# Query and key projections, and their evictions, moved ahead in three of the eight steps of an attention loop

## The chip, the cores and the metric

One NeuronCore of a Trainium2 chip runs the whole program in one launch. The metric is the device time of that launch in microseconds (us), the median of several runs. All durations below are from one profiled execution of the kernel before.

## The reference

Three blocks follow one another on x of 4 batches x 1024 tokens x 128 channels, all in float32:

```python
x = x + 0.5 * ffn(layernorm(x))        # silu(gate) * up, 384 hidden, dequantized int weights
x = x + attn(layernorm(x))
x = x + 0.5 * ffn(layernorm(x))

# attn, 16 heads of 64
h = silu(x @ W1.T + b1) @ W2.T + b2
q, k, v = split(h @ Wg.T + bg)
dots = q @ k.T * 64 ** -0.5
dots = where(j >= i + 64, -inf, dots)  # a query sees the keys up to 63 places after itself
out = softmax(dots) @ v
attn = out @ Wo.T + bo
```

## The kernel before

The change lies in the attention. It runs 32 **turns**, one for each batch and pair of heads (A and B, 64 rows of the array each); the first and the last turn are written out, the 30 between them stand in a loop over two turns. A turn has eight **steps**, one for each tile of 128 queries. The order of the tiles (`at_step`) alternates narrow and wide ones, since the number of keys that a tile sees (`width`) grows with its place:

| step c | 0 | 1 | 2 | 3 | 4 | 5 | 6 | 7 |
|---|---|---|---|---|---|---|---|---|
| keys (width) | 192 | 1024 | 448 | 960 | 320 | 832 | 576 | 704 |
| job for the shared bank 7 | none | v0 | k0 | v1 | k1 | q0 | q1 | none |
| step whose groups are turned (c - 3) | 5 | 6 | 7 | 0 | 1 | 2 | 3 | 4 |
| groups of that step | 4 | 3 | 3 | 1 | 4 | 2 | 4 | 2 |

Every engine has its instructions written out in order, in a function `step` of its own, and starts them in that order; semaphores alone tie the engines together. What one step does, for step c:

- TensorE (PE), `step` at L914: `score` (L844) computes the scores of both heads, with each operand split into a high and a low part and so three matmuls for each head and part of up to 512 keys, into the only score banks there are. It waits for head B's exponentials of step c - 1, which read those banks (L850, L857); in steps 1, 3 and 5 the upper part (bank) can be written before that wait, because the step before it is narrow enough to lie in the lower bank. Then `turn` (L868) transposes the probabilities of step c - 3, four blocks of 128 to a group, the groups in turn into banks 4 and 5: group 0 and 1, called T0 and T1 here, and later T2 and T3. T2 can start once T0 has been copied out. Between T1 and T2 stand `project` (L775), which computes a job of the next turn (k0, k1, q0, q1) or of this one (v0, v1) into bank 7, once the job before it has been read out of that bank (`misc_read`, L826), and in even steps `output` (L833); in the odd steps `attend` (L886, probabilities times values) ends the step.
- VectorE (DVE), `step` at L683: `row_max` (L624) adds the mask and finds the negated maximum of each head; then `take` (L645) copies its groups (in steps 2, 4 and 6 that is T2) out of banks 4 and 5; then `invert` (L640), which waits for the exponentials of this very step; `add_output`; and last `queries_keys_low` (L581), the low part of a query or key projection out of bank 7, which waits for ScalarE's high part.
- ScalarE (ACT), `step` at L492: `take` of its groups 0 and 1 (L478; in steps 2, 4 and 6 both T0 and T1), then `exps` (L469), the exponentials of head A and head B, each after its maximum, then in steps 1, 3, 5 and 7 the attention's output, then `queries_keys` (L407), the high part of the projection out of bank 7, then the group 3.
- GpSimd (POOL) multiplies the probabilities of a step by the reciprocals of their sums (L387), after `invert`; it does this three steps ahead of the transposes.

The high and the low part of one projection are called its two evictions here: `qk_high` and `qk_done` are their semaphores. A job is run in a step's code only if the next turn exists, so the last turn has none of the k and q jobs. In an odd step an engine reaches `queries_keys` after `attention_out`.

```python
    JOBS = {1: "v0", 2: "k0", 3: "v1", 4: "k1", 5: "q0", 6: "q1"}
```

Of the kernel before, what the change touches and what calls it, by code (L numbers as in the profile page):

```python
# [36 lines left out]
def macaron(nc, x, w1t, b1, w2t, b2, wqkvt, bqk, bv, wot, bo, wgatet, wupt, wdownt, out):  # L37
# [34 lines left out]
    JOBS = {1: "v0", 2: "k0", 3: "v1", 4: "k1", 5: "q0", 6: "q1"}  # L72
# [13 lines left out]
    with ExitStack() as ctx:  # L86
# [114 lines left out]
        def taker(c, g):  # L201
            return int(g == 2) if c % 2 else g % 2
# [44 lines left out]
        def back(i, c, lag):  # L247

            return (i, c - lag) if c >= lag else (i - 1, c - lag + STEPS)
# [9 lines left out]
        def job_turn(job, i):  # L259

            return i + 1 if job[0] in "kq" else i - 1 if job in ("o1", "o2", "o3") else i

        def runs(job, carry, more):
            return more if job[0] in "kq" else carry or job not in ("o1", "o2", "o3")
# [139 lines left out]
        def _(act):  # L404
            give_credits(act, "scalar")

            def queries_keys(name, n, r, bank=MISC):  # L407

                kind, j = name[0], int(name[1])
                act.wait_ge(proj_qk.sem, proj_qk.after(name, n))  # L410
                nc.scalar.activation((qt if kind == "q" else kt)[r][0][:, j * BANK:(j + 1) * BANK], banks[:, bank, :], ACT.Identity,  # L411
                                     bias=bslot[r][:, 0:1] if kind == "q" else bslot[r][:, 1:2]).then_inc(qk_high.sem, 1)
# [56 lines left out]
            def exps(c, i):  # L469

                act.wait_ge(turned.sem, turned.after((c, groups[c] - 1), i - 1))
                for h in range(2):
                    act.wait_ge(maxed.sem, maxed.after(f"{c}{HEADS[h]}", i))
                    src = banks[:, SCORE[h]:SCORE[h] + 2, :].rearrange("p b n -> p (b n)")[:, 0:width[c]]
                    nc.scalar.activation(probs[c][:, h, :], src, ACT.Exp, bias=negmax[:, c, h:h + 1],  # L475
                                         accum_out=sums[:, c, h:h + 1]).then_inc(exped.sem, 1)

            def take(c, g, i):  # L478

                act.wait_ge(turned.sem, turned.after((c, g), i))  # L480
                act.wait_ge(attended.sem, attended.after(*two_back(i, c)))
                w = min(4, turns_in[c] - 4 * g)
                nc.scalar.activation(probst[c // 2 % 2][:, 4 * g:4 * g + w, c % 2 * P:(c % 2 + 1) * P],  # L483
                                     banks[:, TRANSPOSED[g % 2], 0:w * P].rearrange("p (t q) -> p t q", q=P), ACT.Copy).then_inc(taken[0].sem, 1)

            def attention_out(p, i):

                act.wait_ge(attended.sem, attended.after(p, i))
                act.wait_ge(wo_done.sem, wo_done.after(f"o{p}", i - 1))
                nc.scalar.activation(attn[:, p, :], banks[:, ATTEND, 0:2 * P], ACT.Copy).then_inc(attn_out.sem, 1)  # L490

            def step(c, i, r, carry=True, more=True):  # L492

                ti, tc = back(i, c, T_LAG)
                turning = carry or c >= T_LAG
                mine = [g for g in range(groups[tc]) if turning and taker(tc, g) == 0]
                for g in mine:
                    if g < 2:
                        take(tc, g, ti)
                exps(c, i)  # L500
                if c in ATTEND_AT and (carry or c >= PV_LAG):
                    for g in mine:
                        if g >= 2:
                            take(tc, g, ti)
                    attention_out(ATTEND_AT[c], i if c >= PV_LAG else i - 1)
                job = JOBS.get(c, "none")
                if job[0] in "kq" and runs(job, carry, more):
                    queries_keys(job, job_turn(job, i), 1 - r if job_turn(job, 0) else r)
                if c not in ATTEND_AT or not (carry or c >= PV_LAG):
                    for g in mine:  # L510
                        if g >= 2:
                            take(tc, g, ti)
# [23 lines left out]
        def _(dve):  # L536
# [87 lines left out]
            def row_max(c, i):  # L624

                lo, hi = hidden_keys[c]
                rows = banks[:, SCORE[0]:SCORE[0] + 4, :].rearrange("p (h b) n -> p h (b n)", h=2)
                dve.wait_ge(scored.sem, scored.after(f"{c}m" if EARLY[c] else f"{c}B", i))

                for heads in ([slice(0, 2)] if lo < BANK < hi else [slice(0, 1), slice(1, 2)]):  # L630
                    here = rows[:, heads, lo:hi]
                    hidden = mask[:, 0:hi - lo].unsqueeze(1).to_broadcast([P, here.shape[1], hi - lo])
                    last = nc.vector.tensor_tensor(here, here, hidden, ALU.add)  # L633
                last.then_inc(masked.sem, 1)
                dve.wait_ge(masked.sem, masked.after(c, i))
                for h in range(2):
                    dve.wait_ge(scored.sem, scored.after(f"{c}{HEADS[h]}", i))
                    nc.vector.tensor_reduce(negmax[:, c, h:h + 1], rows[:, h, 0:hi], AX.X, ALU.max, negate=True).then_inc(maxed.sem, 1)  # L638
# [44 lines left out]
            def step(c, i, r, carry=True, more=True):  # L683

                ti, tc = back(i, c, T_LAG)
                turning = carry or c >= T_LAG
                row_max(c, i)
                for g in range(groups[tc]):
                    if turning and taker(tc, g) == 1:
                        take(tc, g, ti)  # L690
                job = JOBS.get(c, "none")
                if job[0] == "v":
                    evict(job, i, r, carry, more)
                invert(c, i)
                if c in OUTPUTS:
                    evict(OUTPUTS[c], i, r, carry, more)
                if job[0] in "kq":
                    evict(job, i, r, carry, more)

            queries_keys_low("q0", 0, 0, FIRST["q0"])  # L700
# [26 lines left out]
        def _(pe):  # L727
# [47 lines left out]
            def project(name, n, r, bank=MISC):  # L775

                kind, j = name[0], int(name[1])
                if name == "k0":
                    pe.wait_ge(slots.sem, slots.after("b", n))
                w = wslot[r][:, "qkv".index(kind), :]  # L780
                bank = banks[:, bank, :]
                if kind != "v":
                    last = mm(bank, w, hslot[r][:, j * BANK:(j + 1) * BANK], start=True, stop=True)  # L783
                else:
                    for m in range(4):
                        toks = slice((4 * j + m) * P, (4 * j + m + 1) * P)
                        last = mm(bank[:, m * P:(m + 1) * P], hslot[r][:, toks], w, start=True, stop=True)  # L787
                last.then_inc((proj_v if kind == "v" else proj_qk).sem, 1)
# [120 lines left out]
            def turns_of(c, i, gs):  # L909
                for g in gs:  # L910
                    if g < groups[c]:
                        turn(c, g, i)

            def step(c, i, r, carry=True, more=True):  # L914

                ti, tc = back(i, c, T_LAG)
                turning = carry or c >= T_LAG
                attending = c in ATTEND_AT and (carry or c >= PV_LAG)

                score(c, i, r)  # L920
                if turning:
                    turns_of(tc, ti, (0, 1))
                job = JOBS.get(c, "none")
                if c in JOBS and runs(job, carry, more):
                    k = JOB_ORDER.index(job)
                    earlier = [name for name in JOB_ORDER[:k] if runs(name, carry, more)]
                    name, t = (earlier[-1], i) if earlier else (JOB_ORDER[-1], i - 1)
                    misc_read(name, job_turn(name, t))
                    if not carry and k == 0:
                        done(pe, pa.h, "h", CHUNKS - 1)  # L930
                    project(job, job_turn(job, i), 1 - r if job_turn(job, 0) else r)
                if turning and attending:
                    turns_of(tc, ti, (2, 3))
                if attending:
                    attend(ATTEND_AT[c], *((i, r) if c >= PV_LAG else (i - 1, 1 - r)))
                if c in OUTPUTS and runs(OUTPUTS[c], carry, more):
                    output(OUTPUTS[c], job_turn(OUTPUTS[c], i))
                if turning and not attending:
                    turns_of(tc, ti, (2, 3))
# [53 lines left out]
```

## Time and profile before

| | |
|---|---|
| runs of the kernel before | 1331.88 to 1333.56 us, median 1332.67 us (3 runs) |
| the profiled execution | 1333.85 us, of it 1331.2 us from the first instruction to the last (span) |
| granted TensorE clock, mean of the span | 0.997 of 2.4 GHz |
| TensorE matmuls busy | 1275.5 us (96%), 11250 instructions |
| TensorE weight loads busy | 978.4 us (73%) |
| GpSimd busy | 1155.0 us (87%) |
| VectorE busy | 924.5 us (69%) |
| ScalarE busy | 841.9 us (63%) |

The attention begins at 95.7 us of the span, with its first score, and its last score stands at 1259 us; before and after it run the feed-forward blocks. The profile puts every instruction under its line of the kernel, gives its start and duration, and for an engine that stood idle before an instruction it names what ended the wait. A matmul's duration holds a pipelined tail, so that the time that TensorE spends on a group is read from the start of one group to the start of the next.

### The profile page before, as it was taken

Reading aid. Unit: us, or ns where it says so; the run is one execution under the profiler, and the core shown is the slowest. Engines: PE = TensorE matmul, PEld = TensorE weight load, DVE = VectorE, ACT = ScalarE, POOL = GpSimd, SP = SyncE. Lnnn points to the kernel's source line nnn. Section 1 sums busy time; section 2 is a strip of 40 time slices with the busy share of each in tenths; the row PEclk is TensorE's granted clock in tenths of the full one; section 3 lists DMA queues with packets and bytes.
Section 4 is the critical chain, followed back from the end, with each engine's and each line's share of the span. In section 5 each row is a group of like instructions: output and inputs, shape, how many; then the busy total and the mean of one; then the engine's idle time right before and its main releaser. Section 6 shows DMA issues by size and latency. Waiting matters only on the chain.

```text
span 1331.2 us, 34824 instructions
## 1 busy us (share of the span) xinstructions
PE 1275.5 (96%) x11250; PEld 978.4 (73%) x11250; DVE 924.5 (69%) x2110; ACT 841.9 (63%) x1886; POOL 1155.0 (87%) x1090
## 2 busy tenths in 40 slices
PE   4988999999999999999999999999999999999988
PEld 4855777777777777777777777777777777777777
DVE  5856767767677677667677776776676776776755
ACT  2446666666666666666666666666666667666642
POOL 6838998989999999989899989999898999899983
PEclk9998999999999999999999999999999999999999
DMA  4101110000000000000000000000000000000001
GB/s 117 45 0 30 30 30 29 29 11 18 29 29 29 29 29 29 29 29 29 17 11 29 29 29 29 29 29 29 29 29 22 7 29 29 29 29 7 8 17 48
DMA packets 61056, 36.81 MB, mean 28 GB/s; under 512 B 36705, under 2 KB 56034, under 8 KB 61026
## 3 DMA queue, kind: packets, MB, share of 16 engines
q1 hardware_dynamic: 61026, 36.43, 9.3%
q8 instruction: 16, 0.26, 0.1%
q14 instruction: 14, 0.11, 0.0%
HBM read 8.07 MB, written 2.10 MB: 8 GB/s over the span
## 4 chain that ended last, share of the span: by engine, by line
PE 71%; issue 12%; DVE 9%; ACT 5%; POOL 2%; DMA 1%; DVEq 1%; ACTq 0%; SPq 0%; POOLq 0%
PE banks L883 18%; PE banks L861 16%; PE banks L900 15%; PE banks L783 6%; DVE negmax L638 5%; PE banks L841 3%; PE banks L761 3%; PE banks L905 3%; ACT probs L475 3%; DVE banks L633 2%; PE banks L787 2%; PE banks L753 2%; PE banks L754 2%; ACT qt L411 2%; POOL probs L392 1%
## 5 line engine op out<-in xcount | busy, mean ns | idle before, releaser
L392 POOL TENSOR_SCALAR probs<-probs,recips 128x256 f32<-128x256 f32 (+7 forms) x512 | 882.8, 1727 | 114.8 <-DVE recips L643 114.8
L483 ACT ACTIVATE probst<-banks 128x512 f32<-128x512 f32 (+2 forms) x512 | 265.3, 544 | 285.8 <-PE banks L883 285.8
L475 ACT ACTIVATE probs<-banks,negmax 128x320 f32<-128x320 f32 (+7 forms) x512 | 400.3, 789 | 62.2 <-DVE negmax L638 57.1
L638 DVE TENSOR_REDUCE negmax<-banks 128x1 f32<-128x320 f32 (+7 forms) x512 | 393.9, 811 | 32.9 <-PE banks L861 5.2
L883 PE MATMUL banks<-ident,probs 128*128 128x128 f32 x2304 | 331.0, 280 | 2.0 <-DVE probst L650 1.3
L861 PE MATMUL banks<-kt,qt 64*128 64x512 f32 (+4 forms) x2496 | 301.8, 367 | 26.3 <-ACT probs L475 25.6
L883 PEld LDWEIGHTS banks<-ident,probs 128*128 128x128 f32 x2304 | 250.5, 141 | 83.2 <-issue 75.5
L900 PE MATMUL banks<-probst,vs 128*64 128x128 f32 (+1 forms) x3328 | 278.2, 317 | 0.1
L900 PEld LDWEIGHTS banks<-probst,vs 128*64 128x64 f32 x3328 | 201.5, 137 | 84.3 <-issue 34.6
L861 PEld LDWEIGHTS banks<-kt,qt 64*128 64x128 f32 x2496 | 192.7, 185 | 89.3 <-ACT probs L475 44.6
L650 DVE COPY probst<-banks 128x512 f32<-128x512 f32 (+2 forms) x224 | 132.6, 592 | 106.0 <-PE banks L883 105.9
L394 POOL TENSOR_SCALAR ends<-probs,recips 128x64 f32<-128x64 f32 x448 | 200.1, 447 | 0.0
L633 DVE TENSOR_TENSOR banks<-banks,mask 128x128 f32<-128x128 f32 (+2 forms) x480 | 119.4, 292 | 84.1 <-PE banks L861 84.0
L783 PE MATMUL banks<-hslot,wslot 128*128 128x512 f32 x256 | 133.0, 601 | 0.0
L841 PEld LDWEIGHTS banks<-wo_sb,attn 128*128 128x128 f32 x512 | 74.4, 191 | 44.2 <-issue 43.5
L475 ACT ACTIVATION_READ_ACCUMULATOR probs<-banks,negmax 128x1 f32 x512 | 103.8, 203 | 0.0
L643 DVE RECIPROCAL recips<-sums 128x2 f32<-128x2 f32 x256 | 41.3, 161 | 73.8 <-ACT probs L475 71.3
L490 ACT ACTIVATE attn<-banks 128x256 f32<-128x256 f32 x128 | 49.1, 383 | 46.8 <-PE banks L905 44.1
L586 DVE SCALAR_TENSOR_TENSOR qt<-banks,bslot,qt 128x512 fp32r<-128x512 f32 x64 | 47.8, 747 | 44.3 <-ACT qt L411 44.1
L841 PE MATMUL banks<-wo_sb,attn 128*128 (+1 forms) x512 | 77.9, 275 | 0.5 <-ACT attn L490 0.5
L905 PE MATMUL banks<-probst,vh 128*64 128x128 f32 x896 | 70.7, 273 | 0.0
L787 PE MATMUL banks<-wslot,hslot 128*128 128x128 f32 x512 | 68.8, 277 | 0.0
(63 smaller groups left out, 993.2 us busy)
## 6 DMA issues: line engine op xcount, KB each, us to landing
hslot<-h_sb SPq DMA_DIRECT2D x32, 512.0 KB, 3.3
vh<-vs SPq DMA_DIRECT2D x64, 112.0 KB, 2.3
wslot<-in_wqkvt SPq DMA_DIRECT2D x32, 128.0 KB, 2.9
wslot<-wq_sb SPq DMA_DIRECT2D x32, 64.0 KB, 2.5
y<-xres SPq DMA_DIRECT2D x8, 256.0 KB, 2.3
xres<-in_x SPq DMA_DIRECT2D x2, 256.0 KB, 3.8
wo_sb<-in_wot SPq DMA_DIRECT2D x1, 512.0 KB
wq_sb<-in_wqkvt SPq DMA_DIRECT2D x1, 512.0 KB
```

Of the source, the lines that this page charges most:

```text
L392: last = nc.gpsimd.tensor_scalar(here, here, recips[:, c, h:h + 1], None, ALU.mult)
L394: last = nc.gpsimd.tensor_scalar(ends[c][:, half(h)], probs[c][:, h, fulls[c] * P:width[c]], recips[:, c, h:h + 1], None, ALU.mult)
L475: nc.scalar.activation(probs[c][:, h, :], src, ACT.Exp, bias=negmax[:, c, h:h + 1], accum_out=sums[:, c, h:h + 1]).then_inc(exped.sem, 1)
L483: nc.scalar.activation(probst[c // 2 % 2][:, 4 * g:4 * g + w, c % 2 * P:(c % 2 + 1) * P], banks[:, TRANSPOSED[g % 2], 0:w * P].rearrange(" ...
L633: last = nc.vector.tensor_tensor(here, here, hidden, ALU.add)
L638: nc.vector.tensor_reduce(negmax[:, c, h:h + 1], rows[:, h, 0:hi], AX.X, ALU.max, negate=True).then_inc(maxed.sem, 1)
L650: nc.vector.tensor_copy(probst[c // 2 % 2][:, 4 * g:4 * g + w, c % 2 * P:(c % 2 + 1) * P], banks[:, TRANSPOSED[g % 2], 0:w * P].rearrange( ...
L783: last = mm(bank, w, hslot[r][:, j * BANK:(j + 1) * BANK], start=True, stop=True)
L841: last = mm(banks[:, ATTEND, (2 + b) * P:(3 + b) * P], attn[:, j, b * P:(b + 1) * P], w, start=True, stop=True)
L861: last = mm(banks[:, SCORE[h] + b, 0:z - a], qt[r][sq][half(h), at_step[c] * P:(at_step[c] + 1) * P], kt[r][sk][half(h), a:z], start=t == ...
L883: last = nc.tensor.transpose(banks[:, TRANSPOSED[g % 2], (t - 4 * g) * P:(t - 4 * g + 1) * P], block, ident[:])
L900: last = mm(banks[half(h), ATTEND, q], vs[r][:, kb, half(h)], probst[p % 2][:, 2 * kb + h, q], start=(kb == 0), stop=False, skip_group_che ...
```

## The change

In steps with an even number that have a query or key job (2 with k0, 4 with k1, 6 with q1) three things are moved; the odd step 5 with q0 stays as it was. TensorE runs `project` right after `score`, ahead of T0 and T1. ScalarE runs `queries_keys` first in the step, ahead of the copies of T0 and T1 and of the exponentials. VectorE runs `queries_keys_low` right after `row_max`, ahead of its group, of `invert` and of `add_output`. No instruction is added or taken away, and no semaphore changes.

```diff
@@ -494,6 +494,10 @@
                 ti, tc = back(i, c, T_LAG)
                 turning = carry or c >= T_LAG
                 mine = [g for g in range(groups[tc]) if turning and taker(tc, g) == 0]
+                job = JOBS.get(c, "none")
+                ahead = c % 2 == 0 and job[0] in "kq"
+                if ahead and runs(job, carry, more):
+                    queries_keys(job, job_turn(job, i), 1 - r if job_turn(job, 0) else r)
                 for g in mine:
                     if g < 2:
                         take(tc, g, ti)
@@ -503,8 +507,7 @@
                         if g >= 2:
                             take(tc, g, ti)
                     attention_out(ATTEND_AT[c], i if c >= PV_LAG else i - 1)
-                job = JOBS.get(c, "none")
-                if job[0] in "kq" and runs(job, carry, more):
+                if job[0] in "kq" and not ahead and runs(job, carry, more):
                     queries_keys(job, job_turn(job, i), 1 - r if job_turn(job, 0) else r)
                 if c not in ATTEND_AT or not (carry or c >= PV_LAG):
                     for g in mine:
@@ -685,16 +688,19 @@
                 ti, tc = back(i, c, T_LAG)
                 turning = carry or c >= T_LAG
                 row_max(c, i)
+                job = JOBS.get(c, "none")
+                ahead = c % 2 == 0 and job[0] in "kq"
+                if ahead:
+                    evict(job, i, r, carry, more)
                 for g in range(groups[tc]):
                     if turning and taker(tc, g) == 1:
                         take(tc, g, ti)
-                job = JOBS.get(c, "none")
                 if job[0] == "v":
                     evict(job, i, r, carry, more)
                 invert(c, i)
                 if c in OUTPUTS:
                     evict(OUTPUTS[c], i, r, carry, more)
-                if job[0] in "kq":
+                if job[0] in "kq" and not ahead:
                     evict(job, i, r, carry, more)
 
             queries_keys_low("q0", 0, 0, FIRST["q0"])
@@ -918,9 +924,10 @@
                 attending = c in ATTEND_AT and (carry or c >= PV_LAG)
 
                 score(c, i, r)
-                if turning:
+                job = JOBS.get(c, "none")
+                ahead = c % 2 == 0 and job[0] in "kq"
+                if turning and not ahead:
                     turns_of(tc, ti, (0, 1))
-                job = JOBS.get(c, "none")
                 if c in JOBS and runs(job, carry, more):
                     k = JOB_ORDER.index(job)
                     earlier = [name for name in JOB_ORDER[:k] if runs(name, carry, more)]
@@ -929,6 +936,8 @@
                     if not carry and k == 0:
                         done(pe, pa.h, "h", CHUNKS - 1)
                     project(job, job_turn(job, i), 1 - r if job_turn(job, 0) else r)
+                if turning and ahead:
+                    turns_of(tc, ti, (0, 1))
                 if turning and attending:
                     turns_of(tc, ti, (2, 3))
                 if attending:
```

How the order of the instructions moves is shown at three places. The first is TensorE in step 6 of a turn in the loop, from the end of `score` (L861) to T2; L883 is `turn`, L783 `project`, L841 `output`. Before:

```order
L861 MATMUL banks<-kt,qt 128x512 x6
L876 REGISTER_ALU [waits normed]
L883 MATMUL banks<-ident,probs 128x128 [waits taken_scalar]
L883 MATMUL banks<-ident,probs 128x128 x3
L876 REGISTER_ALU [waits normed]
L883 MATMUL banks<-ident,probs 128x128 [waits taken_vector]
L883 MATMUL banks<-ident,probs 128x128 x3
L829 REGISTER_ALU
L783 MATMUL banks<-hslot,wslot 128x512 [waits qk_done]
L838 REGISTER_ALU
L841 ISA [waits attn_out]
L841 MATMUL banks<-wo_sb,attn 128x128 x2
```

Now (the same functions have line numbers higher by 6, L789 is `project`, L889 `turn`):

```order
L867 MATMUL banks<-kt,qt 128x512 x6
L835 REGISTER_ALU
L789 MATMUL banks<-hslot,wslot 128x512 [waits qk_done]
L882 REGISTER_ALU [waits normed]
L889 MATMUL banks<-ident,probs 128x128 [waits taken_scalar]
L889 MATMUL banks<-ident,probs 128x128 x3
L882 REGISTER_ALU [waits normed]
L889 MATMUL banks<-ident,probs 128x128 [waits taken_vector]
L889 MATMUL banks<-ident,probs 128x128 x3
L844 REGISTER_ALU
L847 ISA [waits attn_out]
L847 MATMUL banks<-wo_sb,attn 128x128 x2
```

The projection, with its wait for `qk_done` (the two evictions of q0), has moved from behind eight transposes to ahead of them.

The second place is ScalarE in step 6: L411 is the high part of a projection, L483 a copy of a group, L475 an exponential. The first row is q0's high part, of step 5. Before:

```order
L411 ACTIVATE qt<-banks,bslot 128x512 [waits proj_qk]
L480 REGISTER_ALU
L483 ACTIVATE probst<-banks 128x4x128 [waits attended,turned]
L480 REGISTER_ALU
L483 ACTIVATE probst<-banks 128x4x128 [waits attended,turned]
L473 REGISTER_ALU [waits turned]
L475 ACTIVATE probs,sums<-banks,negmax 128x576 [waits maxed]
L473 REGISTER_ALU
L475 ACTIVATE probs,sums<-banks,negmax 128x576 [waits maxed]
L410 REGISTER_ALU
L411 ACTIVATE qt<-banks,bslot 128x512 [waits proj_qk]
```

Now:

```order
L411 ACTIVATE qt<-banks,bslot 128x512 [waits proj_qk]
L410 REGISTER_ALU
L411 ACTIVATE qt<-banks,bslot 128x512 [waits proj_qk]
L480 REGISTER_ALU
L483 ACTIVATE probst<-banks 128x4x128 [waits attended,turned]
L480 REGISTER_ALU
L483 ACTIVATE probst<-banks 128x4x128 [waits attended,turned]
L473 REGISTER_ALU [waits turned]
L475 ACTIVATE probs,sums<-banks,negmax 128x576 [waits maxed]
L473 REGISTER_ALU
L475 ACTIVATE probs,sums<-banks,negmax 128x576 [waits maxed]
```

The high part of q1 has moved from behind the two exponentials to ahead of the two copies.

The third place is TensorE in step 2, from the end of `score` to T2. Before:

```order
L861 MATMUL banks<-kt,qt 128x448 x5
L883 MATMUL banks<-ident,probs 128x128 [waits taken_scalar,normed]
L883 MATMUL banks<-ident,probs 128x128 x3
L876 REGISTER_ALU [waits normed]
L883 MATMUL banks<-ident,probs 128x128 [waits taken_vector]
L883 MATMUL banks<-ident,probs 128x128 x3
L831 ISA
L779 ISA [waits v_done]
L783 MATMUL banks<-hslot,wslot 128x512 [waits slots]
```

Now:

```order
L867 MATMUL banks<-kt,qt 128x448 x5
L837 ISA
L785 ISA [waits v_done]
L789 MATMUL banks<-hslot,wslot 128x512 [waits slots]
L889 MATMUL banks<-ident,probs 128x128 [waits taken_scalar,normed]
L889 MATMUL banks<-ident,probs 128x128 x3
L882 REGISTER_ALU [waits normed]
L889 MATMUL banks<-ident,probs 128x128 [waits taken_vector]
L889 MATMUL banks<-ident,probs 128x128 x3
```

Here the projection waits for `v_done`, the eviction of v0 in the step before, and it has moved ahead of T0 and T1 too.

## Rows read from the trace of the kernel before

**Rows 1.** Busy times (PE, PEld, DVE, ACT, POOL), clock, DMA of 195 to 1213 us.

```profile
195.00:1213.00 1018.00, 1001.04 (x9161) 763.73 (x9158) 721.88 (x1559) 683.34 (x1561) 922.59 (x834) 1.00 0.09 25
```

**Rows 2.** Who waited for whom, whole span: total us, times, longest.

```profile
PE banks L861 <- ACT probs L475: 25.6, 67, 2.7
```

**Rows 3.** Timeline of TensorE, step 6 and the start of step 7: start, us, group.

```profile
817.48 1.30 PE L861 MATMUL banks<-kt,qt 64*128 64x64 f32 x12
818.71 1.09 PE L883 MATMUL banks<-ident,probs 128*128 128x128 f32 x8
819.64 1.02 PE L783 MATMUL banks<-hslot,wslot 128*128 128x512 f32 x2
820.50 0.61 PE L841 MATMUL banks<-wo_sb,attn 128*128 x4
...
822.21 1.30 PE L861 MATMUL banks<-kt,qt 64*128 64x192 f32 x12 [0.33 <-ACT probs L475]
```

**Rows 4.** Timeline of ScalarE, from q0's high part to step 6's second exponential.

```profile
817.88 0.68 ACT L411 ACTIVATE qt<-banks,bslot 128x512 fp32r<-128x512 f32 x1
819.40 1.08 ACT L483 ACTIVATE probst<-banks 128x512 f32<-128x512 f32 x2 [0.84 <-PE banks L883]
820.60 0.74 ACT L475 ACTIVATE probs<-banks,negmax 128x576 f32<-128x576 f32 x1
...
821.96 0.20 ACT L475 ACTIVATION_READ_ACCUMULATOR probs<-banks,negmax 128x1 f32 x1
822.05 0.69 ACT L411 ACTIVATE qt<-banks,bslot 128x512 fp32r<-128x512 f32 x1
822.62 0.50 ACT L483 ACTIVATE probst<-banks 128x384 f32<-128x384 f32 x1
```

**Rows 5.** Timeline of VectorE, q0's low part to the mask of step 7.

```profile
818.60 0.75 DVE L586 SCALAR_TENSOR_TENSOR qt<-banks,bslot,qt 128x512 fp32r<-128x512 f32 x1 [1.37 <-ACT qt L411]
...
819.81 1.42 DVE L638 TENSOR_REDUCE negmax<-banks 128x1 f32<-128x576 f32 x2
...
823.55 0.49 DVE L633 TENSOR_TENSOR banks<-banks,mask 128x128 f32<-128x128 f32 x2
```

**Rows 6.** Timeline of TensorE, steps 2 and 3 and the start of step 4.

```profile
799.79 1.09 PE L883 MATMUL banks<-ident,probs 128*128 128x128 f32 x8
800.72 1.02 PE L783 MATMUL banks<-hslot,wslot 128*128 128x512 f32 x2
...
802.44 1.58 PE L861 MATMUL banks<-kt,qt 64*128 64x448 f32 x12
...
807.37 0.61 PE L905 MATMUL banks<-probst,vh 128*64 128x128 f32 x8
808.22 0.70 PE L861 MATMUL banks<-kt,qt 64*128 64x320 f32 x6 [0.24 <-ACT probs L475]
```

**Rows 7.** Timelines of ScalarE and VectorE in steps 2 and 3.

```profile
800.48 1.09 ACT L483 ACTIVATE probst<-banks 128x512 f32<-128x512 f32 x2 [0.91 <-PE banks L883]
801.45 0.64 ACT L475 ACTIVATE probs<-banks,negmax 128x448 f32<-128x448 f32 x1
...
802.58 0.22 ACT L475 ACTIVATION_READ_ACCUMULATOR probs<-banks,negmax 128x1 f32 x1
...
804.14 0.49 DVE L633 TENSOR_TENSOR banks<-banks,mask 128x128 f32<-128x128 f32 x2
```

**Rows 8.** Timelines, step 4: second exponential's end on ScalarE, and TensorE's score(5).

```profile
811.42 0.22 ACT L475 ACTIVATION_READ_ACCUMULATOR probs<-banks,negmax 128x1 f32 x1
...
812.05 1.40 PE L861 MATMUL banks<-kt,qt 64*128 64x320 f32 x12
```

**Rows 9.** TensorE in the first turn: timeline, and a window (clock third from last).

```profile
103.02 1.22 PE L861 MATMUL banks<-kt,qt 64*128 64x448 f32 x6 [2.69 <-ACT probs L475]
104.16 2.07 PE L783 MATMUL banks<-hslot,wslot 128*128 128x512 f32 x2
...
103.00:105.00 2.00, 1.98 (x7) 1.08 (x8) 0.83 (x4) 0.00 (x0) 1.64 (x1) 0.59 0.00 0
```

## The prediction

> **What bounds the kernel now.** I read the busy times first. In the loop TensorE has matmuls running for 1001.04 of 1018 us, at a granted clock of 1.00, and GpSimd is next with 922.59 [rows 1]. TensorE is in order and almost never without work, so a stall that it gains is lost time, except where it takes the place of a stall that it has. The list of waits shows which it has: for the scores, until the exponentials before them have left the score banks, 25.6 us in all [rows 2]. The timelines place them: in each turn 0.33 us ahead of score(7) [rows 3] and 0.24 us ahead of score(4) [rows 6]. So score(7) follows the end of exps(6) directly (the record ends at 821.96 + 0.20 = 822.16, the score starts at 822.21 [rows 3, 4]; 0.05 us from an end to what waits for it is used below). Whatever makes exps(6) later makes the turn longer by as much. GpSimd has a tenth of the loop free, and a longer turn gives it more.
>
> **The change part by part.** Nothing is added, so the sum consists of what is later and what is earlier. I walk the three steps with the durations of the rows; all differences are in us of one turn. Three bricks come first. A projection issues for 820.50 - 819.64 = 0.86 on TensorE, and its result is complete 1.02 after its start [rows 3]. T0 can be copied out 819.40 - 818.71 = 0.69 after it starts [rows 3, 4], and T0 with T1 issues for 0.93. On ScalarE the high part holds the engine for 822.62 - 822.05 = 0.57, about 0.60 with its start [rows 4], and the copies of T0 and T1 for 801.45 - 800.48 = 0.97 [rows 7].
>
> *Step 6.* Score(6) has issued at 818.71, where T0 starts now [rows 3]. In the changed order q1 comes there, and it must wait until q0 has been read out of bank 7. The low part of q0 runs from 818.60 for 0.75, to 819.35 [rows 5], and it can't come sooner, since the high part of q0 stands at 817.88, behind the attention's output [rows 4]. Until now T0 and T1 hid this. So q1 starts at about 819.40: a new stall of 0.69. Its result is there at 819.40 + 1.02 + 0.04 = 820.46, and ScalarE, which now must do q1 first, is free at about 821.06. T0 starts at 819.40 + 0.86 = 820.26 and is ready at 820.95, T1 0.45 later; the copies take ScalarE from 821.06 to 822.02, and exps(6) starts there, 1.42 later than its 820.60 [rows 4]. Its maximum is no longer the bound: head A's started at 819.81, both take 1.42, and they end by 821.23 as before [rows 5]. Exps(6) ends at 822.16 + 1.42, and score(7) starts 1.42 late, the old stall of 0.33 included. TensorE's own work would be done by about 822.6 (T3 waits for the copy of T1), so about 1.0 of it is a stall ahead of score(7). **+1.42.**
>
> *Step 7 and on.* VectorE has the low part of q1 behind it by then. It waits in invert for exps(6) at 823.6, adds the output, and comes to the mask of step 7 at about 824.4 instead of 823.55 [rows 5], 0.85 late, less than TensorE's 1.42. The wide exponentials so gain 0.57 on TensorE, but no stall stands behind them that this could remove. **0.**
>
> *Step 2.* K0 waits for v0 alone, which VectorE evicted a step ago: no stall. K0 takes T0's place at 799.79 [rows 6], its result is at ScalarE at 800.85, and ScalarE is free at 801.45; T0, from 800.65, is ready at 801.34. The copies last to 802.42, so exps(2) is 0.97 later than 801.45, and ends at 802.80 + 0.97 = 803.77 [rows 7]. TensorE meanwhile starts the upper part of score(3) at about 802.50, with no wait; 0.70 later, at 803.20, it needs the lower bank, which is released at 803.82. A stall of about 0.6, and score(3), which ended its issue 1.52 after 802.44 [rows 6], ends 0.68 late. On VectorE the low part of k0 is out of the way (0.65 gained) but invert waits 0.97 longer: mask(3) comes at 803.77 + 0.54 = 804.31 instead of 804.14 [rows 7], 0.17 later. So exps(3) ends 0.17 late, at a time when TensorE is 0.68 late: attend ends at 807.37 + 0.61 + 0.68 = 808.66, score(4) can start there instead of at 808.22 [rows 6], and the old stall of 0.24 is gone. **+0.44.**
>
> *Step 4.* The same, with 0.97 on exps(4), whose record ended at 811.42 + 0.22 = 811.64 [rows 8]: now 812.61, released at 812.66. The upper part of score(5) starts at 812.05 and takes about 0.65 for 320 keys [rows 8], so the lower part is due at 812.70. It just fits, with 0.04 to spare; for T3's wait I count **+0.02**.
>
> *The rest.* VectorE's groups, invert and add_output come later, but T0 of the next step and GpSimd, three steps ahead of the transposes, have more than that in hand. DMA queues: none is moved past.
>
> The sum is 1.42 + 0.44 + 0.02 = 1.88 a turn. The jobs run in 31 of the 32 turns: 58.3 us. Against the profiled execution, 1333.85, that gives 1392.1; the median of the runs shown is 1.2 lower, so I forecast **1391 us**, 4.4% slower.
>
> The bounds. Below: of the 1.42 only ScalarE's own 0.60 for the high part stays, and nothing in steps 2 and 4: 0.60 x 31 = 19 us, 1352. Above: nothing fits in steps 2 and 4, and each gives its 0.97 in full: 3.36 x 31 = 104 us, 1437. I take the value of the walk, since every term but the two halves of score(3) and score(5) is a difference of starts that stand in the rows.
>
> A word on the clock. In the first turn TensorE waited 2.69 us for exponentials, and the clock granted behind that was 0.59, so near its lower level (1.2 of 2.4 GHz); two matmuls then took 2.07 instead of 1.02 [rows 9, 3]. In the loop, with stalls of 0.33, it is 1.00 [rows 1]. The new stalls (0.69, 1.0, 0.6) are nearer to the loop's than to 2.69, so I count nothing. The Trainium skill speaks against the change here: by "TensorE: Matmul & The Clock Gate", section "HAM oscillation — how this bites in real kernels", a kernel whose TensorE waits in every pass may fall back to the lower clock each time and pay for it each time. The trace of the first turn agrees that waits do this; by that rule the sum would be the one of the fourth rival below.
>
> **The rivals.**
>
> 1. *Faster.* The low parts of k0, k1 and q1 now hold up the mask of the wide step after them: mask(7) starts where q1's ends, at 823.55, and mask(3) at 804.14 [rows 5, 7]. With them gone, the wide exponentials come up to 0.65 sooner. If exps(6) also ended 0.33 sooner, both old stalls would vanish: 0.57 x 31 = 17.7 us, 1315. It decides at one point: exps(6) must start by 820.3. Against it stands ScalarE's order, by which exps(6) is behind q1 and both copies. 4%.
> 2. *Queued, but mostly hidden.* Only ScalarE's 0.60 in step 6 shows, perhaps with some of the 0.44: 19 to 33 us, 1352 to 1366. This needs q0's eviction to be done when score(6) is, and the rows put it 0.64 behind (819.35 against 818.71). 12%.
> 3. *All three in full*, if the lower halves of score(3) and score(5) have no cover: 1437. For it, only that step 4 fits by 0.04. 6%.
> 4. *The clock falls* in each turn. At half speed the stretch of one projection, T0 and T1 costs their 0.86 + 0.93 again: 1.79 x 31 = 55 us on top, 1446. 5%.
> 5. *It doesn't do what it says*, because the queues overlap anyway and the turn stays as long as it is: 1333. But engines start in order, and the order has changed. 2%.
>
> **How the numbers follow.** The forecast has 71%, mostly within 1370 to 1410. The range 1352 to 1410 takes in rival 2 as well, and leaves out rivals 1, 3, 4 and 5 and what the forecast itself has outside. A measurement of this kernel tells about 0.2% (2.7 us) from no change. Faster by more than that: 4%, rival 1. Within: 2%, rival 5. Slower: 94%.
>
> **What would show it.** In the changed profile TensorE should stand idle ahead of the q1 projection in step 6, about 0.6 to 0.7 us for VectorE's q0, and about 1.0 ahead of score(7) for the exponentials; some 0.6 between the two halves of score(3); none ahead of score(4). VectorE's q1 should follow ScalarE's with no work between, and exps(6) should start at the end of the copies. The turn should last 1.9 us longer. The prediction is wrong if exps(6) starts less than 1 us later against score(6) than now, if step 3 shows no stall, or if the granted clock in the loop is below 1.00.

## The result, and the profile after

The changed kernel takes 1401.76 us (median of 4 runs, 1401.09 to 1402.56), the kernel before 1332.73 us in the runs beside it: a ratio of 1.0516, 95% interval 1.0503 to 1.0529. That is 69.0 us more, 2.23 us for each of the 31 turns that hold the jobs. The forecast was 1391 us, 1.88 a turn.

In the list of waits of the changed kernel, TensorE (PE) waits longer for the exponentials, and for VectorE's part of q0 as well, which is new (columns: total us, times, longest):

```profile
PE banks L867 <- ACT probs L475: 46.3, 67, 2.7
...
PE banks L789 <- DVE qt L589: 19.2, 31, 0.6
```

Against 25.6 us [rows 2], matmuls now stand idle for 46.3 + 19.2 us. These are lower bounds, as a matmul's duration holds a tail that covers the first part of a wait; the starts below are free of it. The clock is no part of it: in the same stretch of the loop as [rows 1] it is again 1.00, and it is the busy time of matmuls (second figure) that fell from 1001.04 to 966.96 of 1018 us, from 98% to 95%.

```profile
195.00:1213.00 1018.00, 966.96 (x8642) 719.02 (x8640) 699.87 (x1470) 638.83 (x1470) 870.88 (x789) 1.00 0.08 25
```

The timeline of TensorE in a turn of the changed kernel, from k0 (L789) in step 2 to score(7) in step 7 (L867 scores, L889 transposes, L847 output). It answers to [rows 6, 8, 3]:

```profile
763.99 1.12 PE L789 MATMUL banks<-hslot,wslot 128*128 128x512 f32 x2
...
766.85 0.88 PE L867 MATMUL banks<-kt,qt 64*128 64x448 f32 x6
768.09 0.96 PE L867 MATMUL banks<-kt,qt 64*128 64x512 f32 x6 [0.36 <-ACT probs L475]
...
772.89 0.71 PE L867 MATMUL banks<-kt,qt 64*128 64x320 f32 x6
773.52 1.12 PE L789 MATMUL banks<-hslot,wslot 128*128 128x512 f32 x2
774.49 1.04 PE L889 MATMUL banks<-ident,probs 128*128 128x128 f32 x8
775.36 0.61 PE L847 MATMUL banks<-wo_sb,attn 128*128 x4
776.01 1.07 PE L889 MATMUL banks<-ident,probs 128*128 128x128 f32 x8
777.00 1.41 PE L867 MATMUL banks<-kt,qt 64*128 64x320 f32 x12
...
782.45 1.30 PE L867 MATMUL banks<-kt,qt 64*128 64x64 f32 x12
784.37 1.13 PE L789 MATMUL banks<-hslot,wslot 128*128 128x512 f32 x2 [0.62 <-DVE qt L589]
...
788.69 1.30 PE L867 MATMUL banks<-kt,qt 64*128 64x192 f32 x12 [0.88 <-ACT probs L475]
```

From one start to another, in us (the sum, 2.28, is this turn's; 2.23 is the whole loss divided by 31):

| stretch | before | after | difference | forecast |
|---|---|---|---|---|
| behind score(2) to score(4) | 8.43 | 8.90 | +0.47 | +0.44 |
| score(4) to score(5) | 3.83 | 4.11 | +0.28 | +0.02 |
| score(5) to score(6) | 5.43 | 5.45 | +0.02 | 0 |
| score(6) to score(7) | 4.73 | 6.24 | +1.51 | +1.42 |

ScalarE in steps 2, 4 and 6 (L411 high part, L483 the copies of T0 and T1, L475 exponentials), which answers to [rows 7, 4]:

```profile
765.15 0.69 ACT L411 ACTIVATE kt<-banks,bslot 128x512 fp32r<-128x512 f32 x1 [1.39 <-PE banks L789]
...
766.69 0.65 ACT L475 ACTIVATE probs<-banks,negmax 128x448 f32<-128x448 f32 x1
...
775.27 1.08 ACT L483 ACTIVATE probst<-banks 128x512 f32<-128x512 f32 x2
...
785.53 0.69 ACT L411 ACTIVATE qt<-banks,bslot 128x512 fp32r<-128x512 f32 x1 [2.00 <-PE banks L789]
786.12 1.08 ACT L483 ACTIVATE probst<-banks 128x512 f32<-128x512 f32 x2
787.07 0.75 ACT L475 ACTIVATE probs<-banks,negmax 128x576 f32<-128x576 f32 x1
...
788.41 0.23 ACT L475 ACTIVATION_READ_ACCUMULATOR probs<-banks,negmax 128x1 f32 x1
```

The order is the one forecast: the high part, then the copies, and the exponentials begin as the copies end. From the end of score(6)'s issue (782.45 + 1.23, with the issue time of 817.48 to 818.71 [rows 3]) to exps(6) there are 3.39 us, where there were 1.89.

VectorE: mask(3), the low part of q0 and mask(6), the low part of q1, mask(7); it answers to [rows 5, 7]:

```profile
768.73 0.49 DVE L636 TENSOR_TENSOR banks<-banks,mask 128x128 f32<-128x128 f32 x2
...
783.56 0.75 DVE L589 SCALAR_TENSOR_TENSOR qt<-banks,bslot,qt 128x512 fp32r<-128x512 f32 x1 [1.66 <-ACT qt L411]
784.23 0.42 DVE L636 TENSOR_TENSOR banks<-banks,mask 128x256 f32<-128x256 f32 x1
...
786.25 0.75 DVE L589 SCALAR_TENSOR_TENSOR qt<-banks,bslot,qt 128x512 fp32r<-128x512 f32 x1
...
789.37 0.49 DVE L636 TENSOR_TENSOR banks<-banks,mask 128x128 f32<-128x128 f32 x2
```

The low part of q0 ends at 783.56 + 0.75 = 784.31, and q1 starts at 784.37 on TensorE, 0.69 behind the end of score(6).

### The profile page after: what moved, and what is told of

Same layout as the page of the kernel before. It is cut to its first block, busy times and chain, and to the rows that moved or that the text cites. A ratio compares the mean times of both kernels' runs of the same rounds, so it can differ in the third digit from the quotient of the medians.

```text
span 1399.6 us, 34824 instructions
## 1 busy us (share of the span) xinstructions
PE 1302.6 (93%) x11250; PEld 977.5 (70%) x11250; DVE 945.9 (68%) x2110; ACT 835.4 (60%) x1886; POOL 1154.0 (82%) x1090
## 4 chain that ended last, share of the span: by engine, by line
PE 76%; ACT 10%; issue 8%; DVE 3%; POOL 1%; DMA 1%; ACTq 1%; SPq 0%; POOLq 0%; DVEq 0%
PE banks L906 19%; PE banks L867 16%; PE banks L889 15%; PE banks L789 9%; ACT probs L475 6%; PE banks L793 4%; PE banks L911 3%; PE banks L767 3%; PE banks L847 2%; ACT probst L483 2%; PE banks L759 2%; DVE qt L589 2%; PE banks L760 2%; ACT qt L411 2%; POOL probs L392 1%
## 5 line engine op out<-in xcount | busy, mean ns | idle before, releaser
L475 ACT ACTIVATE probs<-banks,negmax 128x320 f32<-128x320 f32 (+7 forms) x512 | 400.5, 793 | 22.1 <-DVE negmax L641 18.0
L483 ACT ACTIVATE probst<-banks 128x512 f32<-128x512 f32 (+2 forms) x512 | 265.5, 546 | 219.9 <-PE banks L889 219.9
L867 PE MATMUL banks<-kt,qt 64*128 64x512 f32 (+4 forms) x2496 | 309.8, 370 | 46.3 <-ACT probs L475 46.3
L889 PEld LDWEIGHTS banks<-ident,probs 128*128 128x128 f32 x2304 | 253.2, 141 | 121.1 <-issue 108.7
L889 PE MATMUL banks<-ident,probs 128*128 128x128 f32 x2304 | 329.8, 280 | 4.2 <-DVE probst L653 1.3
L867 PEld LDWEIGHTS banks<-kt,qt 64*128 64x128 f32 x2496 | 190.0, 185 | 116.8 <-ACT probs L475 72.2
L789 PE MATMUL banks<-hslot,wslot 128*128 128x512 f32 x256 | 141.6, 635 | 19.2 <-DVE qt L589 19.2
L475 ACT ACTIVATION_READ_ACCUMULATOR probs<-banks,negmax 128x1 f32 x512 | 107.1, 209 | 0.0
L411 ACT ACTIVATE kt<-banks,bslot 128x512 fp32r<-128x512 f32 x64 | 44.0, 687 | 87.4 <-PE banks L789 87.4
L411 ACT ACTIVATE qt<-banks,bslot 128x512 fp32r<-128x512 f32 x64 | 43.8, 685 | 62.5 <-PE banks L789 62.5
L847 PE MATMUL banks<-wo_sb,attn 128*128 (+1 forms) x512 | 78.2, 275 | 0.5 <-ACT attn L490 0.5
L789 PEld LDWEIGHTS banks<-hslot,wslot 128*128 128x128 f32 x256 | 38.6, 189 | 49.1 <-DVE qt L589 32.7
```

What stands on the lines that cost most here:

```text
L867: last = mm(banks[:, SCORE[h] + b, 0:z - a], qt[r][sq][half(h), at_step[c] * P:(at_step[c] + 1) * P], kt[r][sk][half(h), a:z], start=t == ...
L889: last = nc.tensor.transpose(banks[:, TRANSPOSED[g % 2], (t - 4 * g) * P:(t - 4 * g + 1) * P], block, ident[:])
```

## The experiments

All times are medians against the kernel before in the same comparison (1331.7 to 1332.9 us). Which steps and engines have the new order is set by the value of `ahead` in the three `step` functions (ScalarE, VectorE, TensorE); where the diff names no engine, it is changed in all three.

**Where in the turn.** First, only step 6.

```diff
-                ahead = c % 2 == 0 and job[0] in "kq"
+                ahead = c == 6
```

> Only step 6 has the new order, on all three engines. My theory: a turn's loss lies for two thirds in step 6, where in the changed kernel score(7) starts 6.24 us after score(6) against 4.73 before, so 1.51 x 31 = 47 us over before, 1379 us, with TensorE idle about 0.6 us ahead of q1 and 0.9 us ahead of score(7). Rival: the loss is what every moved eviction costs alike, a third for each of the three steps: 1356 us.

Measured 1378.4 us, ratio 1.0342 (1.0325 to 1.0360), +45.5. And steps 2 and 4 without 6:

```diff
-                ahead = c % 2 == 0 and job[0] in "kq"
+                ahead = c in (2, 4)
```

> Only steps 2 and 4 have the new order. My theory: the remainder, 0.47 us a turn from step 2 to score(4) and 0.28 in step 4, 0.75 x 31 = 23 us, 1356 us, and no idle time of TensorE ahead of q1. Rival (a third for each step): 1379 us.

Measured 1356.44 us, ratio 1.0181 (1.0164 to 1.0198), +23.5. The list of waits of this kernel has no wait of q1 for VectorE. The two sum to 69.0, which is the whole loss: the steps don't help or hurt each other, and step 6 has two thirds of it. An equal price for every step is out.

**The step that should have been free.** Only step 4, priced at 0.02 by the prediction.

```diff
-                ahead = c % 2 == 0 and job[0] in "kq"
+                ahead = c == 4
```

> Only step 4 has the new order. It is the step that the prediction priced at 0.02 us a turn, since score(5) has its upper part for cover. The trace of the changed kernel shows 3.48 us from its k1 to score(5) where it was 3.20 from T0 to score(5). My theory now: this is TensorE's own time (0.10 more for a projection that begins right behind a score, and 0.2 until T2 can start behind the copy of T0, less 0.06), so it is lost: 0.28 x 31 = 8.7 us, 1341 us. Rival, the prediction's term: 0.02 x 31 = 0.6 us, 1333 us.

Measured 1340.78 us, ratio 1.006 (1.0047 to 1.0074), +8.0, or 0.26 a turn. It is not a wait for the exponentials. Two things make it up, as the timeline after shows. The smaller is in the issue times: k1 starts at 773.52 and T0 at 774.49, 0.97 later, where a projection in its old place issued for 0.86, and the eight transposes issue for 0.87 (to 775.36) instead of 0.93. Together that is 0.05. The larger is a wait: T2, which can't start before T0 has been copied out, starts at 776.01, 0.65 behind the output's matmuls, where in the kernel before it was 0.44 (810.64 to 811.08 in its trace). The copies of T0 and T1 start on ScalarE at 775.27, and T2 starts 0.74 behind that. The same distance, to 0.01, stands in two kernels below, in which the copies start earlier and later against the output, so it is T0's copy that holds T2 up. In the kernel before the copies started at 809.54, 1.54 ahead of T2, and nothing waited for them.

**Which engine's move.** TensorE's alone:

```diff
 # step of ScalarE and step of VectorE
-                ahead = c % 2 == 0 and job[0] in "kq"
+                ahead = False
```

> Only TensorE has the new order; ScalarE and VectorE have theirs of before. My theory: it is TensorE's order that makes the exponentials late, since T0 and T1 come 0.86 to 0.96 us later and ScalarE has to copy both first; the evictions ahead of them cost only 0.1 more and hand VectorE 0.65 back ahead of the wide masks. So TensorE alone is worse than the whole change: step 3 about 0.95, step 5 about 0.5, step 6 about 1.4, in all 2.85 x 31 = 88 us, 1421 us. Rival: ScalarE's high part ahead of the exponentials is the cost (0.6 us in each of three steps), and without it most of the loss is gone: under 1375 us.

Measured 1406.63 us, ratio 1.0557 (1.0539 to 1.0575), +73.7: more than the whole change, as expected, and far from the rival's 1375; but less than the 1421 that I gave. TensorE of this kernel, k0 and score(4), k1 and score(5):

```profile
804.25 1.12 PE L789 MATMUL banks<-hslot,wslot 128*128 128x512 f32 x2
...
813.56 0.71 PE L867 MATMUL banks<-kt,qt 64*128 64x320 f32 x6 [0.24 <-ACT probs L475]
814.19 1.13 PE L789 MATMUL banks<-hslot,wslot 128*128 128x512 f32 x2
...
817.53 1.40 PE L867 MATMUL banks<-kt,qt 64*128 64x320 f32 x12
```

From k0 to score(4) it is 9.31, so +0.88 (0.95 expected), and k1 to score(5) 3.34. The stall of 0.5 that I expected ahead of score(6) isn't there. In the kernel before VectorE came to invert, and so to mask(5), only behind its copy of T2 (811.72 for 0.69) and not behind exps(4), which had ended at 811.64 [rows 8], so it had slack there that I had not counted. And ScalarE in step 2:

```profile
805.85 1.08 ACT L483 ACTIVATE probst<-banks 128x512 f32<-128x512 f32 x2 [1.90 <-PE banks L889]
806.82 0.64 ACT L475 ACTIVATE probs<-banks,negmax 128x448 f32<-128x448 f32 x1
```

exps(2) begin 2.57 after k0's start without the high part ahead of them, and 766.69 - 763.99 = 2.70 with it. So ScalarE's eviction costs the exponentials 0.13; the other 0.9 of their delay comes from TensorE's order, through T0 and T1. In step 4 the eviction costs TensorE as well, through T2 (TensorE's output and T2, then ScalarE's copies):

```profile
816.03 0.61 PE L847 MATMUL banks<-wo_sb,attn 128*128 x4
816.53 1.06 PE L889 MATMUL banks<-ident,probs 128*128 128x128 f32 x8
```

```profile
815.79 1.08 ACT L483 ACTIVATE probst<-banks 128x512 f32<-128x512 f32 x2 [2.02 <-PE banks L889]
```

Without k1's high part ahead of them the copies come 0.24 ahead of the output and not 0.09, and T2, again 0.74 behind them, comes 0.50 behind the output and not 0.65. From k1 to score(5) it is 3.34 (3.48 in the changed kernel, 3.20 from T0 to score(5) in the kernel before): so 0.14, half of step 4's loss, is due to ScalarE's move.

Now the evictions alone, with TensorE's order of before:

```diff
 # step of TensorE
-                ahead = c % 2 == 0 and job[0] in "kq"
+                ahead = False
```

> Only the evictions on ScalarE and VectorE are ahead; TensorE has its order of before, with T0 and T1 ahead of the projection. My theory: ScalarE now waits for a projection that comes 0.93 us later than T0, and does the copies and exponentials after it: exps later by 1.9 us in steps 2 and 4 and 1.65 in step 6, the turn longer by about 1.4 + 1.05 + 1.65 = 4.1 us, in all 127 us, 1460 us. Rival: TensorE's order is the whole cost, and the evictions cost nothing, as VectorE gains what ScalarE loses: 1333 to 1345 us.

Measured 1469.54 us, ratio 1.1027 (1.1009 to 1.1046), +136.6. The rival is out by a hundred microseconds. If the evictions are to stand ahead, TensorE's projection must as well; the parts of the change aren't separate costs to be added (73.7 + 136.6 against 69.0 together). This kernel also showed something that no other did, in step 6 of one turn on TensorE (T0 and T1, q1, T2 and T3, score(7), the transposes behind it, score(0)):

```profile
738.99 1.09 PE L889 MATMUL banks<-ident,probs 128*128 128x128 f32 x8
739.92 1.02 PE L789 MATMUL banks<-hslot,wslot 128*128 128x512 f32 x2
...
742.30 0.84 PE L889 MATMUL banks<-ident,probs 128*128 128x128 f32 x6 [0.91 <-ACT probst L483]
...
744.14 2.22 PE L867 MATMUL banks<-kt,qt 64*128 64x192 f32 x12 [0.88 <-ACT probs L475]
746.29 1.11 PE L889 MATMUL banks<-ident,probs 128*128 128x128 f32 x4
...
750.34 0.58 PE L867 MATMUL banks<-kt,qt 64*128 64x192 f32 x6
```

and on ScalarE, the copies of T0 and T1:

```profile
741.57 1.08 ACT L483 ACTIVATE probst<-banks 128x512 f32<-128x512 f32 x2
```

T2 waits here for the copy in plain sight, and starts 742.30 - 741.57 = 0.73 behind the start of the copies.

Score(7) takes 746.29 - 744.14 = 2.15 to issue, where it took 1.23 [rows 3: 822.21, next start 823.44]. The windows around it (columns: PE, PEld, DVE, ACT, POOL busy, then the granted clock) show why:

```profile
740.00:744.00 4.00, 2.35 (x14) 1.46 (x13) 2.87 (x4) 3.01 (x8) 2.66 (x3) 1.00 0.00 0
744.00:745.00 1.00, 0.86 (x8) 0.86 (x10) 0.59 (x2) 0.47 (x2) 0.51 (x1) 0.63 0.00 0
745.00:746.00 1.00, 1.00 (x8) 0.55 (x4) 0.50 (x2) 0.00 (x0) 1.00 (x1) 0.50 0.00 0
```

The clock went to half, its lower level of 1.2 GHz, as score(7) started, behind two stalls that follow closely: TensorE had matmuls running for 2.35 of the 4 us ahead of it. Behind the first turn this happened in eight of the turns. From score(7) to score(0) it is 6.20 us in these (744.14 to 750.34) and 4.67 in one without it (826.76 to 831.43), so that the eight cost 12.2 us. That covers the 9.5 us by which my 1460 was short, and without them the kernel would be at 1457.

**VectorE's move.** The changed kernel with VectorE's order of before:

```diff
 # step of VectorE
-                ahead = c % 2 == 0 and job[0] in "kq"
+                ahead = False
```

> The changed kernel with VectorE's order of before: the low parts of k0, k1 and q1 stand behind invert and the output's addition again, while TensorE's projection and ScalarE's high part are ahead. My theory: VectorE's move is the one part that pays. Without it the masks of the wide steps come 0.65 us later, which shows where the wide exponentials bind score(4), and a little ahead of score(0): like the kernel with TensorE's move alone (1407 us) with exponentials 0.1 us later still, about 1410 to 1418 us. Rival: VectorE's place has no part in it: 1401 us.

Measured 1420.94 us, ratio 1.0656 (1.0641 to 1.0670), 19 us more than the whole change, and 3 us above my upper figure. VectorE's low part of k0 and its mask(3), and TensorE's k0 and score(4):

```profile
817.89 0.74 DVE L589 SCALAR_TENSOR_TENSOR kt<-banks,bslot,kt 128x512 fp32r<-128x512 f32 x1
818.55 0.49 DVE L636 TENSOR_TENSOR banks<-banks,mask 128x128 f32<-128x128 f32 x2
```

```profile
813.17 1.12 PE L789 MATMUL banks<-hslot,wslot 128*128 128x512 f32 x2
...
822.62 0.70 PE L867 MATMUL banks<-kt,qt 64*128 64x320 f32 x6 [0.24 <-ACT probs L475]
```

Mask(3) comes 818.55 - 813.17 = 5.38 behind k0's start, and 768.73 - 763.99 = 4.74 in the changed kernel; score(4) comes 9.45 behind it instead of 8.90. So VectorE's move is the one part of the change that pays: the wide step's mask is 0.64 sooner, worth 0.55 ahead of score(4), or 17 of the 19 us.

**The wait for q0, and a better kernel.** q0's high part can stand ahead of the attention's output in step 5. First in the changed kernel:

```diff
+                if c == 5 and runs(job, carry, more):
+                    queries_keys(job, job_turn(job, i), 1 - r if job_turn(job, 0) else r)
+                if c in ATTEND_AT and (carry or c >= PV_LAG):
                     attention_out(ATTEND_AT[c], i if c >= PV_LAG else i - 1)
-                if job[0] in "kq" and not ahead and runs(job, carry, more):
+                if job[0] in "kq" and not ahead and c != 5 and runs(job, carry, more):
```

> The changed kernel with the same edit. My theory: the wait of q1 for q0's eviction in step 6, 0.69 us with the time to start again, goes nearly whole, since the low part would end at about the end of score(6); everything behind it in step 6 hangs on it: about 0.65 x 31 = 20 us less than the changed kernel, 1382 us. Rival: exps(6) is bound by ScalarE's queue and the maximum and not by q1's start, so the time stays: 1400 us.

Measured 1381.05 us, ratio to the kernel before 1.0373 (1.0358 to 1.0387), some 20 us below the changed kernel. Score(6), q1, score(7) on TensorE:

```profile
807.25 1.30 PE L870 MATMUL banks<-kt,qt 64*128 64x64 f32 x12
808.48 1.12 PE L792 MATMUL banks<-hslot,wslot 128*128 128x512 f32 x2
...
812.80 1.30 PE L870 MATMUL banks<-kt,qt 64*128 64x192 f32 x12 [0.89 <-ACT probs L475]
```

q1 now starts 1.23 behind score(6), with no wait, and score(7) 5.55 behind it instead of 6.24: 0.69 a turn. So that stall was real and worth what it lasted. Then the same edit in the kernel before (the same lines, without `not ahead and`, with the line that sets `job` put ahead of them):

> The kernel before with one edit: in step 5 ScalarE evicts q0's high part ahead of the attention's output, not behind it. My theory: ScalarE is free at 817.03 and the output's matmuls end at 817.55, so the high part costs ScalarE nothing there; VectorE's low part, the mask and the maximum of step 6 come about 0.4 us sooner, and exps(6) starts when the copies of T0 and T1 are done (820.38) instead of at 820.60: 0.2 us a turn, 7 us, 1326 us. Rival: the copies bind anyway, or the attention's output now comes later and holds up TensorE's output in step 6: 1333 us or more.

Measured 1326.24 us, ratio 0.9958 (0.9944 to 0.9972), and thus faster than both kernels, by 5.5 us or 0.4%. ScalarE around it (q0's high part, the attention's output, the copies, exps(6)):

```profile
811.58 0.69 ACT L411 ACTIVATE qt<-banks,bslot 128x512 fp32r<-128x512 f32 x1
812.26 0.38 ACT L490 ACTIVATE attn<-banks 128x256 f32<-128x256 f32 x1
814.07 1.08 ACT L483 ACTIVATE probst<-banks 128x512 f32<-128x512 f32 x2 [1.42 <-PE banks L886]
815.04 0.74 ACT L475 ACTIVATE probs<-banks,negmax 128x576 f32<-128x576 f32 x1
```

and VectorE, with q0's low part and mask(6):

```profile
812.30 0.75 DVE L589 SCALAR_TENSOR_TENSOR qt<-banks,bslot,qt 128x512 fp32r<-128x512 f32 x1 [0.41 <-ACT qt L411]
813.51 0.43 DVE L636 TENSOR_TENSOR banks<-banks,mask 128x256 f32<-128x256 f32 x1 [0.46 <-PE banks L864]
```

The low part ends at 813.05, ahead of the mask, which now waits for the score. exps(6) starts at 815.04, 0.97 behind the start of the copies (as in [rows 7]), and no longer 1.20 as in [rows 4]. From score(6) to score(7) it is 4.50 instead of 4.73.

## Why the prediction was right, and where it was short

*What bounds the kernel.* Right: a delay of exps(6) is a delay of the turn. Score(7) starts 0.05 behind the record's end again (788.41 + 0.23 = 788.64, 788.69).

*Step 6, +1.42.* Right in its mechanism and nearly in size: 1.51. The stall ahead of q1 was forecast at 0.69 and is 0.69; the start of exps(6) is 1.50 later instead of 1.42. The projection in its new place issues for 0.96 where I took the 0.86 of its old place, and ScalarE gets its result 1.16 behind its start (784.37 to 785.53) where I took 1.06; there the missing 0.1 is. The run with q0's eviction moved shows the stall to be worth 0.69 of the step's 1.51.

*Step 7, 0.* Nearly right. Mask(7) came at 789.37, 0.68 behind the start of score(7), where it stood 1.34 behind it before [rows 3, 5]. In the turn of the rows nothing could come of it: score(0) follows score(7) by 4.68 us, and did by 4.69 before. But the rows show one turn of two. In every other turn of the kernel before it was 4.79 or 4.80 (858.66 to 863.45, for one), and in the changed kernel it is 4.68 in these as well. So some 0.1 was gained in every second turn, about 2 us in all; with VectorE's order of before, 4.80 is back (838.40 to 843.20).

*Step 2, +0.44.* Right: +0.47, with a stall between the halves of score(3), and none ahead of score(4). The second half starts 768.09 - 763.99 = 4.10 behind k0's start, where I had 4.03. That the sum is so near is in part luck: attend's last part starts 0.78 later against the same start (799.79 to 807.37 before, 763.99 to 772.35 after) where I had 0.68, but the stall that goes ahead of score(4) is 0.31 by the starts and not the listed 0.24. The mask was worse than forecast: mask(3) comes 4.74 behind k0's start, and came 4.35 behind T0's before (799.79 to 804.14 [rows 6, 7]), so 0.39 later and not 0.17. It did not show, but only some 0.1 was left: exps(3) ended at 772.74, and score(4) started at 772.89.

*Step 4, +0.02.* This is the term that was wrong: it measured 0.28 in the turn of the table, and 0.26 in the run with step 4 alone. I walked only through the waits for the exponentials, and found that they just fit, which they do, and counted T3's wait for a copy; T2's wait for the copy of T0 I put at nothing, and it is 0.21. In its old order T0 was copied long before T2 came; now T0 starts a projection later and ScalarE has k1's high part ahead of its copy. The rest is the issue times, which I took over from the old places of the groups. T2 comes late in step 2 too (0.56 behind the output, 765.82 to 766.38, instead of 0.44), where the stall behind it hides it.

In the turn of the table the forecast was short by 0.40: 0.26 in step 4, 0.09 in step 6, 0.03 in step 2 and 0.02 in step 5. The gain behind score(7) takes some of it back, and 0.35 is left in the time (2.23 against 1.88). The missing term is small beside the whole, which is why the total still came near.

*The clock.* Counting nothing was right here: 1.00 in the loop. But the reason, that stalls of 1 us are nearer to 0.33 than to 2.69, was weaker than I thought, as the kernel with the evictions alone shows: there the clock went to half in some turns behind two stalls of under 1 us each, close together. The Trainium skill ("TensorE: Matmul & The Clock Gate", section "HAM oscillation — how this bites in real kernels") describes a fall in every pass for a kernel whose TensorE waits some 3 to 5 us for DMA in each. The longest wait in the changed kernel's loop is listed as 0.9 us, so its 1.00 doesn't speak against that section; the falls of the kernel with the evictions alone, behind waits that short, are not what it describes.

*The rivals.* The faster one needed exps(6) sooner, and they came later. "Queued, but mostly hidden" fell with the stall ahead of q1. "All three in full" fell in step 4: what is lost there is not 0.97. The fall of the clock did not come in this kernel, and the turn did get longer, so "it doesn't do what it says" is out as well.

## What to carry to other kernels

Before a job is pulled ahead in one engine's queue, name the instruction that now has to wait behind it and follow that one: here the projection was harmless and the two groups of transposes that it pushed back were what ScalarE had to copy before its exponentials. The same walk, made for a wait that an engine really has, also finds the cheap edit: one eviction moved ahead of an instruction that was waiting anyway. And walk every wait that the moved work can reach, not only those that show in the profile: T2's wait for T0's copy never stopped TensorE before, and became the term that the forecast lacked. Changed neighbours alone moved little, 0.05 us a step.

## What the runs showed of the hardware

A projection of two matmuls issues for 0.96 to 0.97 us right behind a score (64 rows of the array) and for 0.86 between transposes and the output (128 rows); the difference lies between its two matmuls, whose starts are 0.54 apart (773.52, 774.06) instead of 0.43 (809.78, 810.21). The eight transposes behind it take 0.87, and 0.93 right behind a score. What comes next counts as well: q0 of step 5, behind transposes but ahead of probabilities times values (64 columns), issues for 0.95 (814.20 to 815.15 in the kernel before), and there it is the second matmul that takes longer (814.63 to 815.15). Whether it is the change between 64 and 128 rows or columns that costs was not tried.

With the evictions alone moved, TensorE's clock fell to half in eight turns behind two waits listed as 0.91 and 0.88 us, which end 1.8 us apart (742.30 and 744.14). In the changed kernel the waits in step 6 are listed as 0.62 and 0.88 us and end 4.3 us apart (784.37 and 788.69), and the clock stayed at 1.00. What in this difference decides is open, and so is why only some turns were hit: score(7) starts 6.38 behind score(6) in all of them.
